# Four graph layers on one Trainium2 core: sums of layers 0 to 2 kept in PSUM, ScalarE's table row moved behind the next tile's hidden row, and layer 3's weighing done in the tile's own turn

## The chip, the cores and the metric

The kernel runs on one core of a Trainium2 chip. The metric is device time in microseconds, the median of the runs of one kernel. The profile is one execution; its times count from the first instruction.

## The reference

Four attention layers over 4096 nodes with 256 features share one sparse, symmetric adjacency matrix (about 9 neighbours a node, the node itself among them). Cut to what matters here:

```python
# each layer: h = relu(layernorm(x)); x = x + layer(h, adj, ...)
# layer 0 (4 heads): Wh = h @ W; e = leaky_relu(s_i[i] + s_j[j], 0.2), only where adj
out = elu(einsum('ijh,jhd->ihd', softmax(e, axis=1), Wh))
# layer 1 (1 head): h = node @ W; the same kind of scores, slope 0.01
out = h + softmax(e) @ node
# layer 2 (4 heads): as layer 0 with biases, no elu
out = einsum('hij,hjf->hif', softmax(S_masked), x_prime)
# layer 3 (4 heads): q, k, v = h @ Wq + bq, h @ Wk + bk, h @ Wv + bv
out = softmax(q @ k.T / 8 + mask) @ v
```

## The kernel before, in words

A first stage (266 us, not touched) turns the matrix into lists of neighbours and sorts the nodes by degree. From then on a tile is 128 nodes, one on each partition, and tile t takes `KS[t]` neighbours a node, from 23 for tile 0 down to 3 for tile 31: 276 in all. Layers 0 to 2 take the tiles in that order, layer 3 in the order `MIXED`, where long and short ones alternate (11, 11, 10, 10, 3, 5, 23, 9, 8, 5, 6, 9, 12, ... neighbours).

Every layer is a pipeline over 32 tiles:

- **POOL** gathers. One indirect DMA (line L749) fetches one neighbour's row for all 128 nodes, so that a layer has 276 of them. They land in a ring in SBUF (`s_ring`), where the tile's own row stands behind them: a tile with k neighbours has c = k + 1 rows. A tile's first gather waits until the tile whose room it takes is summed (semaphore `agg`). In layer 3 POOL also sends finished tiles home (L756), seven tiles behind its gathers, which waits for the tile's end (`x_new`).
- **VectorE (DVE)**, layers 0 to 2: scores (L1268 to L1272); in layer 0 then the places of the neighbours, in layer 1 a test of symmetry; the end of the tile before (`vec_finish`, L1427 to L1433: the sum is added to x) and its statistics (L1044 to L1049); the weights' normalising (L1300, L1307); and `vec_sum`, which multiplies the c rows by their weights (L1395), adds the upper half of the rows to the lower until two are left (L1399), and adds these into `s_half` (L1402). In layer 0 L1440 follows, which adds another product of the tile two before.
- **ScalarE (ACT)**, layers 0 to 2, for tile n: the exponentials (`act_exp`, L939), then `act_row(n-2)` (L916 to L930), which copies the next layer's projection of tile n-2 out of PSUM and stores it to the next layer's table in HBM, then `act_hidden(n-1)` (L877 to L895: layernorm and relu) and `act_turned(n-1)` (L904: copies the transposed row that TensorE made of it). In layer 0 `act_below` stands first.
- **TensorE (PE)**, layers 0 to 2: for each tile a transposition (L1555) and the projection (L1575 to L1586). In layer 2 this is layer 3's projection, k and v (L1575) and then q (L1580, L1581), whose PSUM bank must have been emptied by `act_row` of the tile before.
- **The next layer's first gathers** stand behind two waits: `EARLY` gathers of its first four tiles (24, before layer 3 20) go out when table rows up to tile 27 are stored, and take neighbours from these alone; the rest when all 32 tiles are.
- **Layer 3**: for tile n VectorE multiplies keys and query (`vec_dots`: L1284, L1286 and two small ones, the last L1290), then normalises and weighs tile n-1 (`vec_normal`, `vec_weigh`: L1300 to L1305, L1412 to L1417) and finishes tile n-2 (L1433). ScalarE runs the exponentials of tile n as soon as L1290 is done, then a copy of the query of tile n+2 (L957), and then weighs the first three rows of tile n-1 (`act_spare`, L967). TensorE adds the weighed rows of a tile in PSUM (L1600) and those three last (L1603), which raises `agg`.

All orders are written out by hand; no scheduler moves anything.

Of the kernel before, what the change touches and what calls it, by code (L numbers as in the profile page):

```python
# [9 lines left out]
ALU = mybir.AluOpType  # L10
# [453 lines left out]
class Sparse:  # L464
# [98 lines left out]
        return self.bank(4 if n % 2 == 0 else 6, 0, D)  # L563

    def total_y(self, L, n):
        return self.half[:, n % 2, :] if L.n < 3 else self.bank(2 + n % 2, 0, D)

    def landed(self, L, n):

# [400 lines left out]
    def act_layer(self, e, L):  # L970
        l = L.n + 1
        e.preload_act_table_set("natural_log_exp_and_others")
        if l == 1:
            e.wait_ge(self.ruled, 3 + len(set(KS)))
        if l == 4:
            self.act_asked(e, 0)
            self.act_asked(e, 1)
        for n in range(T):
            if n and l == 1:
                self.act_below(e, n - 1)  # L980
            self.act_exp(e, L, n)
            if l == 4:
                if n + 2 < T:
                    self.act_asked(e, n + 2)
                if n:
                    self.act_spare(e, n - 1)
                continue
            if n > 1:
                self.act_row(e, l, n - 2)
            if n:  # L990
                self.act_hidden(e, l, n - 1)
                self.act_turned(e, l, n - 1)
        if l == 1:
            self.act_below(e, T - 1)
        if l < 4:
            self.act_hidden(e, l, T - 1)
            self.act_row(e, l, T - 2)
            self.act_turned(e, l, T - 1)
            self.act_row(e, l, T - 1)
        else:  # L1000
            self.act_spare(e, T - 1)
# [417 lines left out]
    def vec_finish(self, e, L, n):  # L1419
# [22 lines left out]
    def vec_layer(self, e, L):  # L1442
# [301 lines left out]
```

## Time and profile before

| | |
|---|---|
| median of 3 runs | 1858.07 us (1850.53 to 1858.45) |
| the profiled execution: time, span | 1857.89 us, 1856.1 us |
| busy: POOL, DVE, PE, ACT | 1183.0, 1276.6, 724.0, 638.4 us |
| instructions on DVE, PE, ACT, POOL | 2730, 2660, 2069, 1201 |
| first stage | to 265.6 us |
| layer 0, layer 1, layer 2 (first to last gather) | 265.6 to 634.5, 637.8 to 1006.7, 1007.2 to 1374.9 us |
| layer 3 (first gather to the end) | 1403.9 to 1856.1 us |
| share of the chain that ended last: POOL, "issue" | 53%, 18% |

The busy time of an engine says how much it did, and the idle time before an instruction, with its releaser, what it waited for. "issue" is time between two instructions in which the profile shows no wait. A stage is bound by the engine that never waits in it, which need not be the busiest over the whole span.

### The profile page before, as it was taken

To read this page: it belongs to the slowest core of one execution; us is meant where nothing else is said; L and a number is where in the kernel's file an instruction comes from. 1 tells how busy PE (TensorE), PEld (TensorE's weight loads), DVE (VectorE), ACT (ScalarE), POOL (GpSimd) and SP (SyncE) were. 2 spreads that over 40 slices of the span, in tenths; PEclk is the share of its full clock that TensorE was granted. 3 is DMA by queue.
4 is the path that set the end of the run, shared out by engine and by line. 5 is a ranking of instruction groups with operands and counts; after the bars stand their busy time and mean duration, and the time that the engine had idled before them with its cause. 6 is when DMAs were issued, how large, how long until landed. Compare 5 with 4: busy or idle time off the path is not lost.

```text
span 1856.1 us, 12880 instructions
## 1 busy us (share of the span) xinstructions
PE 724.0 (39%) x2660; PEld 407.7 (22%) x2660; DVE 1276.6 (69%) x2730; ACT 638.4 (34%) x2069; POOL 1183.0 (64%) x1201
## 2 busy tenths in 40 slices
PE   3565500112223312233345134555666233455354
PEld 2443300001111101111122011222222222334243
DVE  2887743978888929666778196677653639668684
ACT  6778500223334511112223123233333222423343
POOL 0000267777777777777777787777744654777774
PEclk9996555555555555555555566666666566776777
DMA  9999789444454464444455644455545665777773
GB/s 354 384 384 364 183 278 169 107 117 119 125 133 129 129 135 110 123 128 124 131 142 135 135 119 141 138 151 152 161 137 158 193 167 160 232 239 223 240 233 101
DMA packets 171212, 328.63 MB, mean 177 GB/s; under 512 B 39918, under 2 KB 82935, under 8 KB 171128
## 3 DMA queue, kind: packets, MB, share of 16 engines
q0 software_dynamic: 65920, 197.88, 39.4%
q1 hardware_dynamic: 82600, 104.48, 17.6%
q10 hardware_dynamic: 22608, 25.40, 4.0%
q8 instruction: 23, 0.38, 0.1%
q14 instruction: 61, 0.50, 0.1%
HBM read 288.94 MB, written 38.72 MB: 177 GB/s over the span
## 4 chain that ended last, share of the span: by engine, by line
POOL 53%; issue 18%; PE 9%; DVE 8%; ACT 6%; DMA 4%; SPq 1%; ACTq 1%; POOLq 0%; DVEq 0%
POOL s_ring L749 50%; PE ps L1575 3%; ACT s_a L804 2%; DMA s_adj<-in_adj_dram 2%; DMA s_ring<-s_tab,s_idx 2%; PE ps L1544 2%; POOL s_pay L736 1%; DVE s_sc L1286 1%; DVE s_ring L1284 1%; POOL out_dram L756 1%; PE ps L1580 1%; SPq L599 1%; PE ps L1600 1%; DVE s_ring L1395 1%; DVE s_ring L1399 1%
## 5 line engine op out<-in xcount | busy, mean ns | idle before, releaser
L749 POOL DMA_INDIRECT s_ring<-s_tab,s_idx x1104 | 1115.6, 1010 | 419.3 <-issue 337.3
L939 ACT ACTIVATE ps<-s_sc,s_least 128x9 f32<-128x9 f32 (+12 forms) x416 | 110.3, 265 | 701.5 <-DVE s_least L1272 461.1
L1395 DVE TENSOR_TENSOR s_ring<-s_ring,ps 128x2304 f32<-128x2304 f32 (+10 forms) x96 | 261.2, 2720 | 3.3
L1399 DVE TENSOR_TENSOR s_ring<-s_ring 128x512 f32<-128x512 f32 (+7 forms) x249 | 234.8, 943 | 8.6
L1555 PE MATMUL ps<-s_ident,s_hb 128*128 128x128 f32 x128 | 43.8, 446 | 415.9 <-ACT s_hb L895 359.9
L1600 PE MATMUL ps<-s_ring,s_ident 128*128 128x256 f32 x366 | 125.2, 511 | 202.9 <-DVE s_ring L1417 202.9
L736 POOL DMA_INDIRECT s_pay<-s_pay_t,s_rank_i x32 | 31.2, 974 | 223.0 <-DVE s_rank_f L1144 213.5
L1284 DVE TENSOR_TENSOR s_ring<-s_ring,ps 128x2304 f32<-128x2304 f32 (+12 forms) x32 | 87.1, 2721 | 123.6 <-DMA s_ring<-s_tab,s_idx 123.2
L1268 DVE SCALAR_TENSOR_TENSOR s_sc<-s_ring 128x36 f32<-128x36 f32 (+20 forms) x96 | 18.4, 192 | 186.9 <-DMA s_ring<-s_tab,s_idx 186.6
L1584 PE MATMUL ps<-s_wx,s_hT 128*128 128x258 f32 (+1 forms) x256 | 134.8, 682 | 30.9 <-ACT s_hT L904 29.8
L1600 PEld LDWEIGHTS ps<-s_ring,s_ident 128*128 128x128 f32 x366 | 92.6, 261 | 232.5 <-issue 214.4
L1555 PE MATMUL ps<-s_ident,s_tb 128*128 128x128 f32 x64 | 22.1, 448 | 304.2 <-ACT s_tb L895 301.9
L1575 PE MATMUL ps<-s_wx,s_hT 128*128 128x512 f32 x128 | 118.9, 1084 | 16.7 <-ACT s_hT L904 16.2
L804 ACT ACTIVATE s_a<-s_adj 128x4096 fp8e4<-128x4096 int32 x32 | 115.4, 3610 | 14.9 <-DMA s_adj<-in_adj_dram 14.8
L1555 PEld LDWEIGHTS ps<-s_ident,s_hb 128*128 128x128 f32 x128 | 18.5, 203 | 445.6 <-ACT s_hb L895 388.7
L967 ACT ACTIVATE s_ring<-s_ring,s_few 128x64 f32<-128x64 f32 x384 | 94.5, 333 | 0.0
L1584 PEld LDWEIGHTS ps<-s_wx,s_hT 128*128 128x128 f32 x256 | 75.2, 324 | 69.0 <-ACT s_hT L904 54.6
L1286 DVE TENSOR_REDUCE s_sc<-s_ring 128x36 f32<-128x2304 f32 (+12 forms) x32 | 87.0, 2720 | 1.1
L1555 PEld LDWEIGHTS ps<-s_ident,s_tb 128*128 128x128 f32 x64 | 9.3, 204 | 326.8 <-ACT s_tb L895 326.8
L939 ACT ACTIVATION_READ_ACCUMULATOR ps<-s_sc,s_least 128x1 f32 x416 | 77.8, 187 | 0.0
L1544 PE MATMUL ps<-s_wx,s_hT 128*128 128x264 f32 x128 | 67.3, 681 | 18.2 <-ACT s_pay_t L865 16.8
L877 ACT ACTIVATE s_stat<-s_stat,s_eps 128x1 f32<-128x1 f32 x96 | 28.2, 294 | 106.0 <-DVE s_stat L1049 80.3
(190 smaller groups left out, 1409.3 us busy)
## 6 DMA issues: line engine op xcount, KB each, us to landing
s_adj<-in_adj_dram SPq DMA_DIRECT2D x32, 2048.0 KB, 16.1
s_ring<-s_tab,s_idx POOLq DMA_INDIRECT x1104, 3.2
s_tab<-s_tb ACTq DMA_DIRECT2D x32, 256.0 KB, 2.5
s_ring<-s_tab SPq DMA_DIRECT2D x32, 256.0 KB, 3.7
s_ring<-s_pay SPq DMA_DIRECT2D x32, 132.0 KB, 2.3
s_tab<-s_tb ACTq DMA_DIRECT2D x32, 132.0 KB, 2.5
s_ring<-s_tab SPq DMA_DIRECT2D x32, 132.0 KB, 2.3
s_tab<-s_tb ACTq DMA_DIRECT2D x32, 129.0 KB, 2.4
```

The costliest lines, as they stand in the source:

```text
L749: e.indirect_dma_start(g[:, k, 0:L.row], None, table, bass.IndirectOffsetOnAxis(ap=self.idx[:, t, k:k + 1], axis=0)).then_inc(self.gat[n % ...
L804: e.activation(self.a8[:, q % 2], self.adj[:, r], ACT.Copy, saturate=False).then_inc(self.conv)
L939: m = e.activation(p[:, :, h], s[:, :, h], ACT.Exp, bias=self.least[:, j, h:h + 1], scale=-1.0, accum_out=self.total[:, j, h:h + 1])
L967: m = e.activation(v, v, ACT.Copy, scale=p[:, k, h:h + 1])
L1284: e.tensor_tensor(keys, keys, wide(self.asked_for(n), 1, k + 1), ALU.mult).then_inc(self.v)
L1286: e.tensor_reduce(s, keys.rearrange("p k (h d) -> p k h d", h=4), AX, ALU.add).then_inc(self.v)
L1395: e.tensor_tensor(v, v, wide(p, 3, L.hd), ALU.mult).then_inc(self.v)
L1399: e.tensor_tensor(g[:, 0:h, :], g[:, 0:h, :], g[:, c - h:c, :], ALU.add).then_inc(self.v)
L1544: x = e.matmul(self.bank(7, 0, cols), self.hT[:, t % 2, k, :], self.wx[:, k, 0:cols], start=(k == 0), stop=(k == 1))
L1575: e.matmul(o, self.hT[:, j, k, :], self.wx[:, k, D:3 * D], start=(k == 0), stop=False)
L1584: x = e.matmul(o[:, 0:cols], self.hT[:, j, k, :], self.wx[:, k, 0:cols], start=(k == 0), stop=(k == 1 and l == 1))
L1600: e.matmul(y, self.ident[:], v, start=(k == SPARED), stop=False)
```

## The change

Three edits, the first on VectorE, the second on ScalarE, the third on VectorE:

1. In layers 0 to 2 the first two weighed rows are written to PSUM bank 2 (`two`, 512 columns), the others stay weighed in the ring. The ring's rows are then added to `two` one pair at a time. Layer 0 joins the two halves at the end; layers 1 and 2 leave them apart, and `vec_finish` adds them to x in two instructions.
2. `act_row(n-2)` stands behind `act_hidden(n-1)` and `act_turned(n-1)`.
3. In layer 3 a tile is `prompt` when the next one has eight gathers or more (19 of 32, the last among them): it is normalised and weighed right behind its own `vec_dots`, and finished behind the `vec_dots` of the next tile. The other 13 keep their order.

```diff
+HEAVY = 8
     def total_y(self, L, n):
-        return self.half[:, n % 2, :] if L.n < 3 else self.bank(2 + n % 2, 0, D)
+        return self.bank(2 if L.n < 3 else 2 + n % 2, 0, D)
+    def two(self):
+        return self.bank(2).rearrange("p (k d) -> p k d", k=2)
# act_layer
-            if n > 1:
-                self.act_row(e, l, n - 2)
             if n:
                 self.act_hidden(e, l, n - 1)
                 self.act_turned(e, l, n - 1)
+            if n > 1:
+                self.act_row(e, l, n - 2)
         if l < 4:
             self.act_hidden(e, l, T - 1)
+            self.act_turned(e, l, T - 1)
             self.act_row(e, l, T - 2)
-            self.act_turned(e, l, T - 1)
             self.act_row(e, l, T - 1)
# vec_sum
-        e.tensor_tensor(v, v, wide(p, 3, L.hd), ALU.mult).then_inc(self.v)
-        while c > 2:
-            e.wait_ge(self.v, vs.up())
-            h = c // 2
-            e.tensor_tensor(g[:, 0:h, :], g[:, 0:h, :], g[:, c - h:c, :], ALU.add).then_inc(self.v)
-            c -= h
-        e.wait_ge(self.v, vs.up())
-        e.tensor_tensor(self.half[:, n % 2, :], g[:, 0, :], g[:, 1, :], ALU.add).then_inc(self.agg)
+        e.tensor_tensor(parted(two), parted(g[:, 0:2, :]), wide(p[:, 0:2], 3, L.hd), ALU.mult).then_inc(self.v)
+        vs.up()
+        v = parted(g[:, 2:c, :])
+        e.tensor_tensor(v, v, wide(p[:, 2:c], 3, L.hd), ALU.mult).then_inc(self.v)
+        vs.up()
+        if c % 2:
+            e.wait_ge(self.v, vs.n)
+            e.tensor_tensor(two[:, 0, :], two[:, 0, :], g[:, c - 1, :], ALU.add).then_inc(self.v)
+            vs.up()
+            c -= 1
+        for a in range(2, c - 2, 2):
+            e.wait_ge(self.v, vs.n)
+            e.tensor_tensor(two, two, g[:, a:a + 2, :], ALU.add).then_inc(self.v)
+            vs.up()
+        e.wait_ge(self.v, vs.n)
+        if L.n:
+            e.tensor_tensor(two, two, g[:, c - 2:c, :], ALU.add).then_inc(self.agg)
+            return
+        e.tensor_tensor(g[:, c - 1, :], two[:, 1, :], g[:, c - 1, :], ALU.add).then_inc(self.v)
+        e.tensor_tensor(two[:, 0, :], two[:, 0, :], g[:, c - 2, :], ALU.add).then_inc(self.v)
+        vs.up()
+        e.wait_ge(self.v, vs.up())
+        e.tensor_tensor(two[:, 0, :], two[:, 0, :], g[:, c - 1, :], ALU.add).then_inc(self.agg)
# vec_finish, layer 1 (layer 2 alike, without total)
-            e.scalar_tensor_tensor(x, y, self.total[:, n % 2, 0:1], x, ALU.mult, ALU.add).then_inc(self.x_new)
+            e.scalar_tensor_tensor(x, y, total, x, ALU.mult, ALU.add).then_inc(self.v)
+            e.wait_ge(self.v, vs.up())
+            e.scalar_tensor_tensor(x, self.two()[:, 1, :], total, x, ALU.mult, ALU.add).then_inc(self.x_new)
+    def prompt(self, n):
+        return n == T - 1 or KS[MIXED[n + 1]] >= HEAVY
# vec_last
             self.vec_dots(e, n)
-            if n:
+            if n and not self.prompt(n - 1):
                 self.vec_normal(e, L, n - 1)
                 self.vec_weigh(e, n - 1)
-            if n > 1:
+            if n > 1 and not self.prompt(n - 2):
                 self.vec_finish(e, L, n - 2)
+            if n and self.prompt(n - 1):
+                self.vec_finish(e, L, n - 1)
+            if self.prompt(n):
+                self.vec_normal(e, L, n)
+                self.vec_weigh(e, n)
```

What this does to the instructions is seen at three places. Line numbers of the changed program are four or more higher.

VectorE before, layer 0, from the normalising of a tile with ten rows to the tile's end:

```order
L1307 TENSOR_TENSOR ps<-ps,s_total 128x40
L1395 TENSOR_TENSOR s_ring<-s_ring,ps 128x10x256
L1399 TENSOR_TENSOR s_ring<-s_ring 128x5x256
L1399 TENSOR_TENSOR s_ring<-s_ring 128x2x256
L1399 TENSOR_TENSOR s_ring<-s_ring 128x256
L1402 TENSOR_TENSOR s_half<-s_ring 128x256
L1440 TENSOR_TENSOR s_xs<-s_xs,ps 128x256
```

VectorE in the changed program, layer 0, the same place of such a tile (L1311 is the normalising, L1466 what was L1440):

```order
L1311 TENSOR_TENSOR ps<-ps,s_total 128x40
L1399 TENSOR_TENSOR ps<-s_ring,ps 128x512
L1402 TENSOR_TENSOR s_ring<-s_ring,ps 128x8x256
L1411 TENSOR_TENSOR ps<-ps,s_ring 128x512 x3
L1417 TENSOR_TENSOR s_ring<-ps,s_ring 128x256
L1418 TENSOR_TENSOR ps<-ps,s_ring 128x256
L1421 TENSOR_TENSOR ps<-ps,s_ring 128x256
L1466 TENSOR_TENSOR s_xs<-s_xs,ps 128x256
```

One multiplication and four additions have become two and six, and no addition reads two rows of SBUF any more.

ScalarE before, near the end of layer 2: the exponentials of tile 29 (six rows), and what stands behind them:

```order
L939 ACTIVATE ps,s_total<-s_sc,s_least 128x6 x4
L921 ACTIVATE s_tb<-ps 128x256
L922 ACTIVATE s_tb<-ps 128x512
L928 DMA s_tab<-s_tb 128x512
L930 DMA s_q<-s_tb 128x256
L877 ACTIVATE s_stat<-s_stat,s_eps 128x1
L879 ACTIVATE s_stat<-s_stat 128x1
L881 ACTIVATE s_stat<-s_stat 128x1
L895 ACTIVATE s_hb<-s_xs,s_stat 128x256
L904 ACTIVATE s_hT<-ps 128x256
```

ScalarE in the changed program, the same place:

```order
L943 ACTIVATE ps,s_total<-s_sc,s_least 128x6 x4
L881 ACTIVATE s_stat<-s_stat,s_eps 128x1
L883 ACTIVATE s_stat<-s_stat 128x1
L885 ACTIVATE s_stat<-s_stat 128x1
L899 ACTIVATE s_hb<-s_xs,s_stat 128x256
L908 ACTIVATE s_hT<-ps 128x256
L925 ACTIVATE s_tb<-ps 128x256
L926 ACTIVATE s_tb<-ps 128x512
L932 DMA s_tab<-s_tb 128x512
L934 DMA s_q<-s_tb 128x256
```

The copies and stores of tile 27 (two copies, two DMAs) have moved behind the hidden row of tile 28 and the copy of its transposition.

VectorE before, layer 3, the tile with 13 rows (place 12; place 11 in front of it has 10 rows, place 10 seven):

```order
L1284 TENSOR_TENSOR s_ring<-s_ring,ps 128x13x256
L1286 TENSOR_REDUCE s_sc<-s_ring 128x52
L1288 TENSOR_TENSOR s_sc<-s_sc,s_gap 128x48
L1290 TENSOR_REDUCE s_least<-s_sc 128x4
L1300 RECIPROCAL s_total<-s_total 128x4
L1304 TENSOR_TENSOR s_few<-ps,s_total 128x12
L1305 TENSOR_TENSOR ps<-ps,s_total 128x28
L1417 TENSOR_TENSOR s_ring<-s_ring,ps 128x4x256
L1417 TENSOR_TENSOR s_ring<-s_ring,ps 128x3x256
L1433 TENSOR_TENSOR s_xs<-s_xs,ps 128x256
```

VectorE in the changed program, the same tile (L1459 is the finish):

```order
L1288 TENSOR_TENSOR s_ring<-s_ring,ps 128x13x256
L1290 TENSOR_REDUCE s_sc<-s_ring 128x52
L1292 TENSOR_TENSOR s_sc<-s_sc,s_gap 128x48
L1294 TENSOR_REDUCE s_least<-s_sc 128x4
L1459 TENSOR_TENSOR s_xs<-s_xs,ps 128x256
L1304 RECIPROCAL s_total<-s_total 128x4
L1308 TENSOR_TENSOR s_few<-ps,s_total 128x12
L1309 TENSOR_TENSOR ps<-ps,s_total 128x40
L1436 TENSOR_TENSOR s_ring<-s_ring,ps 128x7x256
L1431 TENSOR_TENSOR s_ring<-s_ring,ps 128x3x256
L1433 TENSOR_REDUCE s_half<-s_ring 128x256
```

Before, the seven rows weighed here are those of place 11 (4 and 3), and the finish at the end is that of place 10. Now the finish comes first and is that of place 11, and the ten rows weighed behind it (7 and 3) are the tile's own.

## Rows read from the trace of the kernel before

**Rows 1.** Busy times by stage: stretch, us, PE, PEld, DVE, ACT, POOL (x instructions), clock, DMA.

```profile
265.60:634.50 368.90, 77.72 (x168) 41.01 (x168) 283.93 (x655) 113.66 (x466) 285.03 (x276) 0.50 0.55 137
1007.20:1374.90 367.70, 175.14 (x336) 70.36 (x336) 237.71 (x418) 109.87 (x428) 283.87 (x276) 0.63 0.53 144
```

**Rows 2.** Waits of POOL over the whole span: us in total, times, longest.

```profile
POOL s_ring L749 <- issue: 337.3, 1097, 3.4
POOL s_ring L749 <- DMA s_q<-s_tb: 42.3, 2, 29.0
```

**Rows 3.** The gathers' group on the page, and a stretch of the timeline (start, us).

```profile
L749 POOL DMA_INDIRECT s_ring<-s_tab,s_idx x1104 | 1115.6, 1010 | 419.3 <-issue 337.3
...
1209.00 2.82 DVE L1395 TENSOR_TENSOR s_ring<-s_ring,ps 128x2560 f32<-128x2560 f32 x1
...
1209.90 0.95 POOL L749 DMA_INDIRECT s_ring<-s_tab,s_idx  x1 [0.30 <-issue]
...
1211.86 2.68 DVE L1399 TENSOR_TENSOR s_ring<-s_ring 128x1280 f32<-128x1280 f32 x3
...
1212.40 1.76 POOL L749 DMA_INDIRECT s_ring<-s_tab,s_idx  x1 [0.30 <-issue]
```

**Rows 4.** VectorE's groups by form: times, busy us, mean ns of one, idle before.

```profile
L1402 DVE TENSOR_TENSOR s_half<-s_ring 128x256 f32<-128x256 f32 x96 | 40.8, 425 | 3.3
L1440 DVE TENSOR_TENSOR s_xs<-s_xs,ps 128x256 f32<-128x256 f32 x32 | 13.3, 415 | 4.7 <-ACT s_tb L916 4.7
L1417 DVE TENSOR_TENSOR s_ring<-s_ring,ps 128x512 f32<-128x512 f32 x15 | 9.9, 684 | 0.2
L1307 DVE TENSOR_TENSOR ps<-ps,s_total 128x40 f32<-128x40 f32 x8 | 1.7, 208 | 0.3
```

**Rows 5.** Waits of VectorE from 313.0 to 632.3 us (layer 0, tiles 0 to 28).

```profile
DVE s_sc L1268 <- DMA s_ring<-s_tab,s_idx: 26.4, 14, 4.0
```

**Rows 6.** Timeline at the change from layer 0 to layer 1.

```profile
634.31 0.33 ACTq L925 DMA_DIRECT2D s_tab<-s_tb  x1
...
637.82 0.38 ACT L904 ACTIVATE s_hT<-ps 128x256 f32<-128x256 f32 x1 [0.78 <-PE ps L1555]
637.84 1.59 POOL L749 DMA_INDIRECT s_ring<-s_tab,s_idx  x1 [3.37 <-issue]
```

**Rows 7.** Timeline of ScalarE near the end of layer 2.

```profile
1358.77 0.38 ACT L921 ACTIVATE s_tb<-ps 128x256 f32<-128x256 f32 x1 [4.69 <-PE ps L1581]
...
1362.80 0.38 ACT L904 ACTIVATE s_hT<-ps 128x256 f32<-128x256 f32 x1 [0.78 <-PE ps L1555]
...
1369.01 0.38 ACT L921 ACTIVATE s_tb<-ps 128x256 f32<-128x256 f32 x1 [4.68 <-PE ps L1581]
```

**Rows 8.** Timeline of POOL: layer 3's first gather, and its twenty-first.

```profile
1403.91 0.95 POOL L749 DMA_INDIRECT s_ring<-s_tab,s_idx  x1 [29.03 <-DMA s_q<-s_tb]
...
1442.07 0.94 POOL L749 DMA_INDIRECT s_ring<-s_tab,s_idx  x1 [13.29 <-DMA s_q<-s_tb]
```

**Rows 9.** Timeline in layer 3 around the end of one tile's `vec_dots`.

```profile
1700.50 0.28 ACT L939 ACTIVATE ps<-s_sc,s_least 128x9 f32<-128x9 f32 x1 [7.74 <-DVE s_least L1290]
...
1701.99 2.96 ACT L967 ACTIVATE s_ring<-s_ring,s_few 128x64 f32<-128x64 f32 x12
...
1709.52 1.46 PE L1603 MATMUL ps<-s_ring,s_ident 128*128 128x256 f32 x6
```

**Rows 10.** VectorE in layer 3: waits from 1452.3 us, the first, the longest of the rest, the last.

```profile
DVE s_ring L1284 <- DMA s_ring<-s_tab,s_idx: 123.2, 19, 32.6
DVE s_xs L1433 <- PE ps L1603: 9.1, 3, 3.6
...
1452.28 3.35 DVE L1284 TENSOR_TENSOR s_ring<-s_ring,ps 128x3072 f32<-128x3072 f32 x1 [32.58 <-DMA s_ring<-s_tab,s_idx]
...
1533.89 6.55 DVE L1284 TENSOR_TENSOR s_ring<-s_ring,ps 128x6144 f32<-128x6144 f32 x1 [28.44 <-DMA s_ring<-s_tab,s_idx]
...
1843.48 0.42 DVE L1433 TENSOR_TENSOR s_xs<-s_xs,ps 128x256 f32<-128x256 f32 x1 [2.67 <-PE ps L1603]
```

More of the change, by code:

```diff
@@ L1388, in vec_sum @@
         vs, g, p = self.vs, self.rows(L, n)[:, :, 0:D], self.scores(L, n)[1]
-        c = KS[L.order[n]] + 1
+        c, two = KS[L.order[n]] + 1, self.two()
+        parted = lambda a: a.rearrange("p k (h d) -> p k h d", h=L.heads)
         if L.n == 1:
@@ L1393, in vec_sum @@
             e.wait_ge(self.normal, self.normals(L, n))
-        v = g.rearrange("p k (h d) -> p k h d", h=L.heads)
-        e.tensor_tensor(v, v, wide(p, 3, L.hd), ALU.mult).then_inc(self.v)
-        while c > 2:
-            e.wait_ge(self.v, vs.up())
-            h = c // 2
-            e.tensor_tensor(g[:, 0:h, :], g[:, 0:h, :], g[:, c - h:c, :], ALU.add).then_inc(self.v)
-            c -= h
+        e.tensor_tensor(parted(two), parted(g[:, 0:2, :]), wide(p[:, 0:2], 3, L.hd), ALU.mult).then_inc(self.v)
[19 more added lines that the diff above has]
+        vs.up()
         e.wait_ge(self.v, vs.up())
-        e.tensor_tensor(self.half[:, n % 2, :], g[:, 0, :], g[:, 1, :], ALU.add).then_inc(self.agg)
+        e.tensor_tensor(two[:, 0, :], two[:, 0, :], g[:, c - 1, :], ALU.add).then_inc(self.agg)
     def vec_weigh(self, e, n):
@@ L1430, in vec_finish @@
         elif L.n == 1:
-            e.scalar_tensor_tensor(x, y, self.total[:, n % 2, 0:1], x, ALU.mult, ALU.add).then_inc(self.x_new)
+            total = self.total[:, n % 2, 0:1]
+            e.scalar_tensor_tensor(x, y, total, x, ALU.mult, ALU.add).then_inc(self.v)
+            e.wait_ge(self.v, vs.up())
+            e.scalar_tensor_tensor(x, self.two()[:, 1, :], total, x, ALU.mult, ALU.add).then_inc(self.x_new)
+        elif L.n == 2:
+            e.tensor_tensor(x, x, y, ALU.add).then_inc(self.v)
+            e.wait_ge(self.v, vs.up())
+            e.tensor_tensor(x, x, self.two()[:, 1, :], ALU.add).then_inc(self.x_new)
         else:
@@ L1475, in vec_last @@
             self.vec_dots(e, n)
-            if n:
+            if n and not self.prompt(n - 1):
                 self.vec_normal(e, L, n - 1)
                 self.vec_weigh(e, n - 1)
-            if n > 1:
+            if n > 1 and not self.prompt(n - 2):
                 self.vec_finish(e, L, n - 2)
-        self.vec_normal(e, L, T - 1)
-        self.vec_weigh(e, T - 1)
-        self.vec_finish(e, L, T - 2)
+            if n and self.prompt(n - 1):
[3 more added lines that the diff above has]
+                self.vec_weigh(e, n)
+        if not self.prompt(T - 2):
+            self.vec_finish(e, L, T - 2)
         self.vec_finish(e, L, T - 1)
```

## The prediction

> **What bounds the kernel now.** I read the busy times by stage first. In layer 0 and in layer 2 POOL runs 276 gathers in 368.9 and 367.7 us with 285.0 and 283.9 us of busy time [rows 1]; layer 1 reads like layer 0. Then POOL's waits: nearly all of its idle time is "issue", 337.3 us in 1,097 pieces of 0.3, which is the price of the next gather, not a wait [rows 2]. So layers 0 to 2 run at POOL's pace. A free gather takes 0.95 us and 0.30 of issue, 1.25 together [rows 3]; 276 of them are 344.6 us. What is above that is in long gathers: 1,104 took 1115.6 us [rows 3], which is 72 more than 1,104 x 0.945. The timeline shows when. A gather that starts while L1395 multiplies (one operand in SBUF, one in PSUM) takes 0.95; the one that started at 1212.40, half a microsecond into the three L1399 additions (both operands in SBUF), took 1.76 [rows 3]. The first of the three (1280 columns, 1.49 us at 960 columns a us and 0.15 fixed) ends at 1213.35, the gather 0.81 later. I laid all gathers over the instruction that VectorE runs 0.13 us after their start: under L1399 112 of 132 are long, and each ends 0.82 us after that addition; under L1395 none of 206. Some 68 of the 72 us lie under L1399 and L1402, 24 us of it in each of layers 0 and 1 and 23 in layer 2.
>
> One other place costs POOL time before layer 3. Between layers 2 and 3 it waits 29.03 and 13.29 us for stored table rows [rows 8], 42.3 in all [rows 2].
>
> **Edit 1, the sums.** On POOL it takes away what holds the gathers: the additions read one operand from PSUM. The form "PSUM from PSUM and SBUF" exists before, as L1307 [rows 4], and none of the 9 gathers over it was long. I take 70 of 72 us as gone; layer 0's L1429 (two SBUF operands) keeps about 1.
>
> On VectorE it costs. An operand in PSUM is no dearer: 256 columns take 415 ns with it and 425 without [rows 4], 512 take 684 [rows 4]. L1307, which writes PSUM, takes 208 ns for 40 columns [rows 4]: 166 fixed, where the 684 hold 151. The Trainium skill, "VectorE: DVE Perf Modes", its section on the TRN2 errata, gives an operation from PSUM 62 cycles more of fixed cost than one from SBUF; at its 0.96 GHz that would be 65 ns each and, over some 200 additions up to tile 28, 13 us more in layer 0. The rows show no such difference. The sum goes by the rows. Ten rows before: 2.82 for the multiplication, 2.68 for three additions [rows 3], 0.42 for L1402, some 6.0 with gaps. After, in layer 0: 0.68 and 2.28 (8 rows, 0.15 + 8 x 0.267), three times 0.68, three times 0.42, with gaps 6.6; two pairs do not wait for each other and overlap by 0.12, so +0.3. Twenty-four rows give +1.4, thirteen +0.7, six +0.1. Over tiles 0 to 28 that is +12.8 us in layer 0 and +10.8 in layers 1 and 2 (second addition in the finish included).
>
> Layer 2 has room for it (VectorE busy 238 of 368 us [rows 1]), and layer 1 nearly as much. Layer 0 has not (284 of 369 [rows 1], much of the rest at its start). VectorE starts its first tile at 313.0, 18 us behind the gathers, and up to tile 29's scores (632.3) it waited for gathers 26.4 us [rows 5] of 319.3. With 12.8 more work and no waits that stretch is 305.2 us: tile 29 starts at 618.2, and POOL, done at 610, waits. **Layer 0 becomes VectorE's.**
>
> **Edit 2, ScalarE's order.** It moves two things in opposite ways. The row of tile 27, for which the next layer's first gather waits, now stands behind hidden and turned row of tile 28. In layer 0 its DMA was issued at 634.31, 3.5 us before POOL's first gather of layer 1 (637.84), and the copy L904 that will precede it ended at 638.20 [rows 6]: 4.1 us later. So layer 1 starts at 618.2 + (638.4 - 632.3) + 3.5 = 627.8, where it was 637.8: 10 us gained of the 24. POOL then has 24 early gathers (30 us) before it needs the last rows, which are there. Layer 1: 344.6 us, then a wait of about 3 for tile 27's row (2.7 later by the same count, where POOL arrived just in time): layer 2 starts at 975.5, before 1007.2.
>
> Near the end of layer 2 the old order is a ring: copy of tile n-2's projection, hidden row n-1, its transposition, 5.8 us of projection on PE (1363.18 to 1369.01), and again the copy, which waits 4.69 for it; 10.24 us a tile [rows 7], where the gathers need 8.7 to 3.8. This ring is why POOL waits 42.3 us. In the new order the copy comes when the projection is already done, and PE goes on at once: 5.7 + 0.78 + 0.38 = 6.9 us a tile [rows 7]. From tile 27 on this is a little slower than the gathers. Its row arrives about 5 us after POOL's last gather of layer 2, the last row 1.5 us after the 20 early ones. So 42.3 becomes about 6.5. Layer 3's twenty-first gather then goes out at 975.5 + 344.6 + 5 + 25 + 1.5 = 1351.6, before 1442.1: **90 us ahead**.
>
> **Edit 3, layer 3.** What is queued behind what decides it. `vec_finish(n-1)` now stands before `vec_normal(n)` and waits until tile n-1 is summed. That needs `act_spare(n-1)`, which ScalarE still runs behind the exponentials of tile n, and these wait for `vec_dots(n)`. So the finish cannot start until dots(n) is over and then exponentials, query copy and spare are: 1700.50 to 1704.95, 4.45 us (4.4 to 4.6 in 25 of the 31 tiles that have such a pair), then three matmuls of 1.46 together [rows 9]: 6.1 us in which VectorE stands still. Before, normalising and weighing the last tile covered it; now nothing does. This happens for 18 tiles (all prompt ones but the last): 110 us. Behind it stand the tile's own weighing and all later dots.
>
> VectorE's layer 3 from its first dots (1452.28) to its last finish (1843.48) was 391.2 us, of which it waited 123.2 - 32.6 = 90.6 for gathers and 9.1 for sums [rows 10], so 291.5 of work. New: 291.5 + 110 + 1.5 (first exponentials) + 25 for tile 6 (its ring space comes free when tile 2 is summed, so the 28.4 [rows 10] stay nearly whole) + 5 at the end = 433. A tile with nine rows then takes VectorE some 14 us (twice 2.55 for the dots and 0.4 for the small ones, 6.1, 0.4 for the finish, twice 0.95 and 0.4 for the weighing) against 10.0 for its 8 gathers and one DMA home, so no further wait for gathers hides in it. **Layer 3 becomes VectorE's, 42 us longer.** Ring space freed earlier brings nothing, since POOL no longer leads.
>
> **Sum.** 1351.6 + 10.2 (first landing) + 433 + 12.6 (last finish to the end) = 1807.4 us span, 49 less than 1856.1. The profiled execution took 1.8 more than its span and lies 0.2 below the median of the runs, so I forecast 1809 us.
>
> **Rivals.**
> - *The finish does not stand in layer 3* (ScalarE's part done earlier than I read it). Layer 3 stays POOL's at best: 42 less, 1767. Against it: the order of the three engines. 8%.
> - *The gathers stay held* (an addition with one SBUF operand still takes what a gather reads): the 70 us stay, VectorE's additions are more, only the end of layer 2 gains some 36, layer 3 loses 42, and the stretch before loses a few: about 1870, slower than before. It decides as soon as more than two thirds of the 72 us stay. Against it: 9 short gathers over L1307, 206 over L1395. 6%.
> - *PSUM operands are dearer than the rows say*, as by the rule above. Every 0.05 us on an addition is 10 us in layer 0, while layers 1 and 2 hide it; layer 3 is untouched. No row before shows 512 columns written to PSUM; the bounds from the nearest ones are 0 (L1440 against L1402) and 0.015 (L1307's fixed part), and only a price outside them makes this case: at 0.1 us, 1829. 9%. By the 62 cycles of the Trainium skill ("VectorE: DVE Perf Modes", the TRN2 errata) it would be 1822.
> - *The reorder on ScalarE pays little* because PE's projection slows or tile 27's row comes later than I count: 42 stays half or whole, 1825 to 1845. 8%.
>
> **How the numbers follow.** My forecast as a whole has 69%, with its own range 1792 to 1826: layer 0 +-6, end of layer 2 +-5, layer 3 +-12 (each finish +-0.6). The range 1782 to 1840 leaves out the first two rivals and the worst of the last. A change within 0.5% (1849 to 1867) can hardly be told from none. Faster by over 0.5%: 0.90; within: 0.04; slower: 0.06.
>
> **What would show it.** Long gathers gone in layers 0 to 2 (276 in 285 us of busy time becomes 261). In layer 0 no wait of VectorE for gathers and one of some 18 us of POOL before layer 1. Table row waits before layer 3 of about 5 and 1.5. In layer 3 L1459 with about 18 waits of 6 us for PE's last matmuls, VectorE's dots no longer waiting. It is wrong if those waits are missing, or if gathers over L1411 are long.

## The result, and the profile after

The changed kernel takes 1834.43 us (median of 4 runs, 1831.8 to 1836.44) where the kernel before takes 1857.61 beside it: a ratio of 0.9883, 95% interval 0.9855 to 0.991. That is 23 us less. I had forecast 1809, 49 less. The sign and the stated range (1782 to 1840) held. The gain is a little under half of what I forecast, and the time lies outside the range of the forecast itself (1792 to 1826).

Each time below stands beside that of the kernel before, taken with it; where that is 2135 to 2155 us in place of 1856 to 1858, instructions come late (the last section), so that such a time is compared with its neighbour alone and only waits and durations are read from its trace.

In the page's groups of the changed kernel (busy us, mean ns of one, idle before) the first two rows answer to [rows 3, 4], the third to [rows 10]:

```profile
L753 POOL DMA_INDIRECT s_ring<-s_tab,s_idx x1104 | 1046.3, 948 | 446.4 <-issue 346.8
...
L1411 DVE TENSOR_TENSOR ps<-ps,s_ring 128x512 f32<-128x512 f32 x246 | 171.9, 699 | 8.5
...
L1459 DVE TENSOR_TENSOR s_xs<-s_xs,ps 128x256 f32<-128x256 f32 x32 | 13.4, 418 | 143.7 <-PE ps L1637 143.6
```

The 1,104 gathers have a mean of 948 ns, the free gather's length: of the 72 us of holding 3 are left. The busy times of layers 0 and 2, in the columns of [rows 1]:

```profile
266.20:611.50 345.30, 74.86 (x162) 39.43 (x162) 286.81 (x735) 107.67 (x441) 261.47 (x276) 0.50 0.58 145
975.20:1321.30 346.10, 173.70 (x367) 70.10 (x368) 256.85 (x518) 119.44 (x463) 262.32 (x276) 0.67 0.57 156
```

POOL's 276 gathers take 345 and 346 us where they took 369 and 368 [rows 1], with 261 and 262 us of busy time. The starts of layers 1, 2 and 3 and layer 3's twenty-first gather, in POOL's timeline:

```profile
626.82 0.94 POOL L753 DMA_INDIRECT s_ring<-s_tab,s_idx  x1 [15.35 <-issue]
...
975.21 0.94 POOL L753 DMA_INDIRECT s_ring<-s_tab,s_idx  x1 [3.42 <-DMA s_tab<-s_tb]
...
1324.85 0.94 POOL L753 DMA_INDIRECT s_ring<-s_tab,s_idx  x1 [3.52 <-DMA s_q<-s_tb]
...
1349.84 0.94 POOL L753 DMA_INDIRECT s_ring<-s_tab,s_idx  x1 [0.31 <-issue]
```

I had 627.8, 975.5 and, for the last, 1351.6. POOL stands 15.35 us at the end of layer 0, because that layer is VectorE's now (from 313 to 618 us VectorE waits for no gather, where it waited 26.4 us [rows 5]), and the waits of 29.03 and 13.29 us [rows 8] are 3.52 and 0.31. Up to here the forecast is within 2 us, and the kernel is 92.2 us ahead. The rest is lost in layer 3. Its waits of VectorE (us in total, times, longest), and a stretch of the timeline that answers to [rows 9]:

```profile
DVE s_xs L1459 <- PE ps L1637: 143.6, 22, 9.3
DVE s_ring L1288 <- DMA s_ring<-s_tab,s_idx: 48.8, 2, 26.6
```

```profile
1665.40 0.22 DVE L1294 TENSOR_REDUCE s_least<-s_sc 128x4 f32<-128x36 f32 x1
1665.65 0.28 ACT L943 ACTIVATE ps<-s_sc,s_least 128x9 f32<-128x9 f32 x1 [13.52 <-DVE s_least L1294]
...
1666.83 0.36 ACT L961 ACTIVATE ps<-s_ring 128x256 f32<-128x256 f32 x1
1667.14 2.96 ACT L971 ACTIVATE s_ring<-s_ring,s_few 128x64 f32<-128x64 f32 x12
1670.15 2.93 PE L1637 MATMUL ps<-s_ring,s_ident 128*128 128x256 f32 x6 [6.67 <-ACT s_ring L971]
1673.11 0.42 DVE L1459 TENSOR_TENSOR s_xs<-s_xs,ps 128x256 f32<-128x256 f32 x1 [7.50 <-PE ps L1637]
```

The chain is the one that I described: dots of the next tile, its exponentials, a query copy, ScalarE's three rows (4.45 us from 1665.65 to 1670.10), the three matmuls, the finish. But the matmuls take 2.93 us, not 1.46, and the finish waits 7.50, not 6.1. All 18 prompt tiles show 2.93; 17 of their waits are 7.24 to 7.54 us, one is 9.28, 135.5 together. VectorE's layer 3, from its first dots (1359.91) to its last finish (1820.15), is 460.2 us where I had 433 and where it was 391.2.

### The profile page after: what moved, and what is told of

Its sections match the earlier page's. It is cut to its first block, busy times and chain, and to the rows that moved or that the text cites. A ratio compares the mean times of both kernels' runs of the same rounds, so it can differ in the third digit from the quotient of the medians.

```text
span 1833.3 us, 13149 instructions
## 1 busy us (share of the span) xinstructions
PE 720.6 (39%) x2660; PEld 412.1 (22%) x2660; DVE 1307.3 (71%) x2999; ACT 636.9 (35%) x2069; POOL 1113.8 (61%) x1201
## 4 chain that ended last, share of the span: by engine, by line
DVE 31%; POOL 29%; issue 15%; ACT 9%; PE 8%; DMA 5%; SPq 2%; ACTq 0%; POOLq 0%; DVEq 0%
POOL s_ring L753 27%; DVE s_sc L1290 4%; DVE s_ring L1288 4%; DVE s_ring L1402 4%; DVE ps L1411 3%; PE ps L1637 3%; ACT s_ring L971 3%; ACT s_a L808 3%; SPq L603 2%; DMA s_adj<-in_adj_dram 2%; PE ps L1578 2%; DVE s_ring L1436 2%; DMA s_ring<-s_tab,s_idx 2%; POOL s_pay L740 2%; DVE ps L1399 1%
## 5 line engine op out<-in xcount | busy, mean ns | idle before, releaser
L753 POOL DMA_INDIRECT s_ring<-s_tab,s_idx x1104 | 1046.3, 948 | 446.4 <-issue 346.8
L1402 DVE TENSOR_TENSOR s_ring<-s_ring,ps 128x1792 f32<-128x1792 f32 (+10 forms) x96 | 209.2, 2179 | 0.0
L1411 DVE TENSOR_TENSOR ps<-ps,s_ring 128x512 f32<-128x512 f32 x246 | 171.9, 699 | 8.5
L1634 PE MATMUL ps<-s_ring,s_ident 128*128 128x256 f32 x366 | 125.5, 512 | 114.2 <-DVE s_ring L1436 114.2
L1637 PE MATMUL ps<-s_ring,s_ident 128*128 128x256 f32 x192 | 75.2, 550 | 160.4 <-ACT s_ring L971 160.4
L1634 PEld LDWEIGHTS ps<-s_ring,s_ident 128*128 128x128 f32 x366 | 95.9, 268 | 147.3 <-issue 127.5
L1288 DVE TENSOR_TENSOR s_ring<-s_ring,ps 128x2304 f32<-128x2304 f32 (+12 forms) x32 | 86.9, 2716 | 49.1 <-DMA s_ring<-s_tab,s_idx 48.8
L1459 DVE TENSOR_TENSOR s_xs<-s_xs,ps 128x256 f32<-128x256 f32 x32 | 13.4, 418 | 143.7 <-PE ps L1637 143.6
L1609 PE MATMUL ps<-s_wx,s_hT 128*128 128x512 f32 x128 | 104.7, 965 | 15.2 <-ACT s_hT L908 14.7
L1637 PEld LDWEIGHTS ps<-s_ring,s_ident 128*128 128x128 f32 x192 | 50.1, 274 | 178.5 <-ACT s_ring L971 169.6
```

What stands on the lines that cost most here:

```text
L753: e.indirect_dma_start(g[:, k, 0:L.row], None, table, bass.IndirectOffsetOnAxis(ap=self.idx[:, t, k:k + 1], axis=0)).then_inc(self.gat[n % ...
L1288: e.tensor_tensor(keys, keys, wide(self.asked_for(n), 1, k + 1), ALU.mult).then_inc(self.v)
L1402: e.tensor_tensor(v, v, wide(p[:, 2:c], 3, L.hd), ALU.mult).then_inc(self.v)
L1411: e.tensor_tensor(two, two, g[:, a:a + 2, :], ALU.add).then_inc(self.v)
L1609: e.matmul(o, self.hT[:, j, k, :], self.wx[:, k, D:3 * D], start=(k == 0), stop=False)
L1634: e.matmul(y, self.ident[:], v, start=(k == SPARED), stop=False)
```

## The experiments

**Edits 1 and 2 without 3** (layer 3 in the order of before):

```diff
     def vec_last(self, e, L):
         for n in range(T):
             self.vec_dots(e, n)
-            if n and not self.prompt(n - 1):
+            if n:
                 self.vec_normal(e, L, n - 1)
                 self.vec_weigh(e, n - 1)
...
```

> The changed kernel with layer 3's order of before (edits 1 and 2 alone). If edit 3 costs what the trace after shows (layer 3 from its first dots to its last finish 460 us where it was 391), this kernel is faster than both: 21st gather of layer 3 at about 1350, then 10.2 + 391 + 12.6, span 1764, time 1766. If instead layer 3 became longer because it starts with POOL earlier or because POOL's gathers there meet something new, the order of before would not help and the time stays near 1834.

For the second run:

> The same kernel as the first (edits 1 and 2 alone), once more, since on that chip the kernel before took 2138 us where it had 1858, with stretches in which VectorE got an instruction only every 0.7 us. If the kernel before runs at 1858 here, layer 3's order of before gives 1766 with edits 1 and 2. If the kernel before is at 2138 again, it is again near 2120.

Measured: 1765.79 us beside 1856.48, ratio 0.9509 (0.9489 to 0.953); the first run was 2119.89 beside 2137.86. VectorE's waits in layer 3:

```profile
DVE s_ring L1288 <- DMA s_ring<-s_tab,s_idx: 116.4, 19, 27.8
DVE s_xs L1459 <- PE ps L1633: 8.5, 3, 3.0
```

They are those of [rows 10]: gathers lead again, and the sums are waited for three times. The twenty-first gather went out at 1351.88, and the last finish ended 399.8 us later (401.8 before, 470.7 in the changed kernel). So edit 3 turns a gain of 91 us into one of 23, and the step that sized edits 1 and 2 (90 us) was right.

**Edit 3 without 1 and 2** (the kernel before with `prompt` and the new `vec_last`):

> The kernel before with edit 3 alone. If layer 3's new order makes VectorE stand 7.5 us at 18 finishes whatever comes ahead, layer 3 is 460 us here too: 1442 + 10 + 460 + 13 = 1925 span, time 1927. By the prediction's own sum (6.1 us a finish, 433) it would be 1900. If edit 3 only hurts together with edits 1 and 2, it is near 1858.

Measured: 2223.9 us beside 2137.86, ratio 1.0418 (1.037 to 1.0465), so the time where the kernel before takes 1857 us stays open. The waits can be read; two of VectorE's finishes in layer 3:

```profile
1721.86 0.42 DVE L1434 TENSOR_TENSOR s_xs<-s_xs,ps 128x256 f32<-128x256 f32 x1 [7.51 <-PE ps L1612]
...
1739.32 0.42 DVE L1434 TENSOR_TENSOR s_xs<-s_xs,ps 128x256 f32<-128x256 f32 x1 [7.51 <-PE ps L1612]
```

The 7.5 us are there without edits 1 and 2 (14 of the waits are 7.24 to 7.54). They are a price of the order alone. Ten other waits are shorter or longer than that, up to 24 us.

**Edit 1 without 2 and 3:**

> The kernel before with edit 1 alone. Theory: gathers of layers 0 to 2 free (0.95 us), layer 1 starts near 624, layer 2 near 969; then the ring of 10.24 us a tile at the end of layer 2 stays and takes some 12 of the 23 us back there; 21st gather of layer 3 near 1393, time 1809 (49 less than before). POOL's wait for table rows grows from 42 to over 50. Rival: the ring takes all of it back, since it began before the gathers were held: 1820 to 1830.

For the two runs after it, the last the one that counts:

> The kernel before with edit 1 alone. Where the kernel before takes 1858: gathers of layers 0 to 2 free, layer 1 starts near 624, layer 2 near 969, the ring of 10.24 us a tile at the end of layer 2 stays and takes some 12 of the 23 us back there, 21st gather of layer 3 near 1393, 1809. Rival, the ring takes all of layer 2's gain back: 1820 to 1830. Where the kernel before takes 2138, it is near 2156.

> The kernel before with edit 1 alone. Where the kernel before takes 1858: gathers of layers 0 to 2 free, layer 1 starts near 624, layer 2 near 969, the ring of 10.24 us a tile at the end of layer 2 stays and takes some 12 of the 23 us back there, 21st gather of layer 3 near 1393, 1809. Rival, the ring takes all of layer 2's gain back: 1820 to 1830. Where the kernel before takes 2138, it is near 2156.

Measured: 1798.06 us beside 1856.44, ratio 0.9688 (0.9671 to 0.9706); twice before 2155.83 and 2154.67 beside 2138 and 2137. POOL's waits for table rows before layer 3:

```profile
1341.83 0.95 POOL L752 DMA_INDIRECT s_ring<-s_tab,s_idx  x1 [28.22 <-DMA s_q<-s_tb]
...
1379.98 0.94 POOL L752 DMA_INDIRECT s_ring<-s_tab,s_idx  x1 [13.42 <-DMA s_q<-s_tb]
```

Layers 1 and 2 start at 620.51 and 966.57, as expected within 4 us, but the twenty-first gather goes out 13 us earlier than I expected: the waits are those of [rows 8] to within 1 us, so the faster gathers did not run further into ScalarE's and TensorE's ring at the end of layer 2. My count of a loss of 12 us there was wrong. Edit 1 is worth 58 us and edit 2 on top of it 32 (1798 to 1766, both beside 1856).

**Edit 2 without 1 and 3:**

> The kernel before with edit 2 alone. Theory: layers 1 and 2 start 4 and some 7 us later, the wait for table rows before layer 3 falls from 42 to about 6, 21st gather near 1415, time 1831. Rival: PE's projection or the hidden row stays the ring and the wait stays above 20: 1845 or more.

Measured: 2100.49 us beside 2137.86, ratio 0.9814 (0.9765 to 0.9863): faster, but its size where the kernel before takes 1857 us is open. POOL's waits for table rows before layer 3 are 45.2 us in this run, so it does not show the fall to 6 us that I expected. The runs beside 1856 us show it: 41.6 us with edit 1 alone, 3.9 with edits 1 and 2.

**The running sums in SBUF.** The changed kernel, the same instructions, the sums in `s_half`:

```diff
     def total_y(self, L, n):
-        return self.bank(2 if L.n < 3 else 2 + n % 2, 0, D)
+        return self.half[:, 0, :] if L.n < 3 else self.bank(2 + n % 2, 0, D)
     def two(self):
-        return self.bank(2).rearrange("p (k d) -> p k d", k=2)
+        return self.half[:]
```

> The changed kernel with the two running sums in SBUF (s_half) in place of PSUM bank 2; the same instructions, both operands of each addition in SBUF again. If two SBUF operands are what holds a gather, gathers over L1411 are long again, less than before since each addition is only 0.7 us long: 30 to 60 us of busy time above the free gathers in layers 0 to 2, of which layer 0 hides its part; time 1850 to 1865. If only the length and shape of the old additions held them, gathers stay at 0.95 and the time at 1834.

Measured: 2192.62 us beside 2134.95, ratio 1.0255 (1.0206 to 1.0303); whether it takes 1850 to 1865 us where the kernel before takes 1857 stays open. The gathers can be read. POOL's and VectorE's groups, and the timeline of additions and gathers in layer 0:

```profile
L753 POOL DMA_INDIRECT s_ring<-s_tab,s_idx x1104 | 1073.5, 972 | 764.2 <-issue 387.7 <-PE ps L1637 134.3 <-DVE s_half L1415 89.4
L1411 DVE TENSOR_TENSOR s_half<-s_half,s_ring 128x512 f32<-128x512 f32 x246 | 170.6, 693 | 33.6 <-DVE s_half L1411 18.9 <-issue 3.7 <-DVE s_half L1406 3.2
```

```profile
426.50 1.42 DVE L1411 TENSOR_TENSOR s_half<-s_half,s_ring 128x512 f32<-128x512 f32 x2
426.76 1.25 POOL L753 DMA_INDIRECT s_ring<-s_tab,s_idx  x1 [0.30 <-issue]
428.11 0.69 DVE L1411 TENSOR_TENSOR s_half<-s_half,s_ring 128x512 f32<-128x512 f32 x1 [0.20 <-issue]
428.31 1.31 POOL L753 DMA_INDIRECT s_ring<-s_tab,s_idx  x1 [0.30 <-issue]
```

Gathers over L1411 are long again, 69 of 99, and each ends 0.82 us after the addition that it started under. In the changed kernel a like stretch of layer 0 has four additions in a row and every gather at 0.95:

```profile
394.00 2.90 DVE L1411 TENSOR_TENSOR ps<-ps,s_ring 128x512 f32<-128x512 f32 x4
395.11 0.94 POOL L753 DMA_INDIRECT s_ring<-s_tab,s_idx  x1 [0.30 <-issue]
396.36 0.95 POOL L753 DMA_INDIRECT s_ring<-s_tab,s_idx  x1 [0.30 <-issue]
```

None of the 136 gathers over L1411 is long in the changed kernel, and none of 103 in the first run of edits 1 and 2 alone (2119.89), so late instructions are not the reason. The second operand's place is what frees the gathers, not the shape of the additions. The excess over 0.95 us in layers 0 to 2 is 25 us, under the 30 to 60 that I expected, against 70 before: an addition of 0.69 us holds a gather less long than one of 1.49. By the Trainium skill, "SBUF — State Buffer", the section on who interferes with whom, an instruction of VectorE with two SBUF inputs contends with an instruction of GpSimd that reads SBUF; the trace agrees, as far as the gather is one, since its indices (`s_idx`) lie in SBUF. The rows also price the sum's place itself: 699 ns in PSUM against 693 here, and 433 against 426 for L1421, with nothing else changed. That is 6 to 7 ns. The Trainium skill, "VectorE: DVE Perf Modes", its section on the TRN2 errata, which the prediction weighed, has 62 cycles more for an operation from PSUM, an estimate of 65 ns; the trace does not agree.

**ScalarE's three rows at once.** The changed kernel, with ScalarE weighing them behind a prompt tile's own exponentials:

```diff
                 if n + 2 < T:
                     self.act_asked(e, n + 2)
-                if n:
+                if n and not self.prompt(n - 1):
                     self.act_spare(e, n - 1)
+                if self.prompt(n):
+                    self.act_spare(e, n)
                 continue
...
-        else:
-            self.act_spare(e, T - 1)
```

> The changed kernel with ScalarE weighing the first three rows of a prompt tile behind its own exponentials, ahead of those of the next tile. Theory: a finish then finds its sum ready (no waits at L1459), what stays is 19 waits of 1.5 us for the exponentials ahead of the normalising (28 us); VectorE needs some 350 and POOL leads; ring room comes free earlier by one tile's dots, so 1735 to 1766, about 1750. If the prediction's reading of the order were wrong and the waits had another cause, L1459 waits stay.

For the three runs after it, the last the one that counts:

> The changed kernel with ScalarE weighing the first three rows of a prompt tile behind its own exponentials, ahead of those of the next tile; once more, on a chip where the kernel before should take 1858. Theory: a finish then finds its sum ready (no waits at L1459), what stays is 19 waits of 1.5 us for the exponentials ahead of the normalising (28 us); VectorE needs some 350 and POOL leads; ring room comes free earlier by one tile's dots, so 1735 to 1766, about 1750. If the prediction's reading of the order were wrong and the waits had another cause, L1459 waits stay and the time is near 1834.

> The changed kernel with ScalarE weighing the first three rows of a prompt tile behind its own exponentials, ahead of those of the next tile. Where the kernel before takes 1858: no waits at L1459, 19 waits of 1.4 us for the exponentials at L1304 instead (28 us), POOL leads layer 3 again, 1735 to 1766, about 1750. Rival, the waits at L1459 have another cause: near 1834. Where the kernel before takes 2138, it is at 2120 to 2128 as twice before and tells nothing of the size.

> The changed kernel with ScalarE weighing the first three rows of a prompt tile behind its own exponentials, ahead of those of the next tile. Where the kernel before takes 1858: no waits at L1459, 19 waits of 1.4 us for the exponentials at L1304 instead (28 us), POOL leads layer 3 again, 1735 to 1766, about 1750. Rival, the waits at L1459 have another cause: near 1834. Where the kernel before takes 2138 it tells nothing of the size.

Measured: 1753.94 us beside 1856.79, ratio 0.9449 (0.9433 to 0.9465); three times before 2120.29, 2128.65 and 2124.86 beside 2135 to 2139. The end of one tile's dots in layer 3:

```profile
1566.79 0.26 DVE L1294 TENSOR_REDUCE s_least<-s_sc 128x4 f32<-128x60 f32 x1
1566.96 0.41 DVE L1459 TENSOR_TENSOR s_xs<-s_xs,ps 128x256 f32<-128x256 f32 x1
...
1568.50 0.18 DVE L1304 RECIPROCAL s_total<-s_total 128x4 f32<-128x4 f32 x1 [1.13 <-ACT ps L943]
...
1568.92 2.97 ACT L971 ACTIVATE s_ring<-s_ring,s_few 128x64 f32<-128x64 f32 x12 [0.25 <-DVE s_few L1308]
...
1576.67 1.46 PE L1637 MATMUL ps<-s_ring,s_ident 128*128 128x256 f32 x6
```

The finish (L1459) finds its sum ready and starts at once; what stays is the wait of 1.13 us for the exponentials. Over layer 3 the waits at L1459 fall from 143.6 to 10.9 us, and those for the exponentials at L1304 are ten of 0.3 to 1.4 us, 9.2 together, where I expected 19 and 28 us. The three matmuls come right behind TensorE's other rows and take 1.46. VectorE waits for gathers again (91.8 us at L1288), and the ring's waits of POOL fall from 85.1 to 19.6 us. One edit on ScalarE is worth 80 us, and the prompt order, which cost 69, now gains 12 against the order of before (1765.79).

**TensorE kept busy.** The changed kernel, with 12 more matmuls into an unused bank for each prompt tile from the third on:

```diff
+        if n > 1 and n < T - 1 and self.prompt(n):
+            for k in range(12):
+                if k == 6:
+                    e.wait_ge(self.scored, 3 * T + n + 2)
+                e.matmul(self.bank(5, 0, D), self.ident[:], g[:, SPARED, D:2 * D], start=True, stop=True)
         e.wait_ge(self.spared, n + 1)
```

> The changed kernel with 12 matmuls more for each prompt tile, into an unused PSUM bank: six behind the weighed rows, six when the next tile's dots are done, ahead of the last three. They only keep TensorE busy. If the prediction's finish wait was too small because TensorE, idle for 6 to 10 us, runs the last three matmuls at its lower clock (2.93 us where the row had 1.46), L1637 falls back to 1.46 and each of 18 waits from 7.5 to 6.0: 27 us less, 1807. If the clock isn't the cause, L1637 stays at 2.93 and the time at 1834 or above.

For the two runs after it:

> The changed kernel with 12 matmuls more for each prompt tile into an unused PSUM bank, six behind the weighed rows, six when the next tile's dots are done. Where the kernel before takes 1858: the last three matmuls (L1642) 1.56 us in place of 2.93, the finish waits 6.1 in place of 7.5 for most of 18 tiles, 1834 less 18 x 1.4 = 1809, the forecast. If the wait's size has nothing to do with TensorE's clock, 1834 or more. Where the kernel before takes 2138, only the durations can be read.

> The changed kernel with 12 matmuls more for each prompt tile into an unused PSUM bank. Where the kernel before takes 1858: the last three matmuls (L1642) 1.56 us in place of 2.93, the finish waits 6.1 in place of 7.5 for most of 18 tiles, 1834 less 18 x 1.4 = 1809, the forecast. If the wait's size has nothing to do with TensorE's clock, 1834 or more. Where the kernel before takes 2138, only the durations can be read.

Measured: 2214.08 us beside 2143.7, ratio 1.0334 (1.027 to 1.0397); twice before 2211.68 and 2210.31 beside 2135. Whether it takes the time to 1809 is open. The durations are plain. Tile 1 has no added matmuls, tile 2 has them (L1639); the last three matmuls are L1642:

```profile
1710.26 2.93 PE L1642 MATMUL ps<-s_ring,s_ident 128*128 128x256 f32 x6 [6.34 <-ACT s_ring L971]
1713.22 0.42 DVE L1459 TENSOR_TENSOR s_xs<-s_xs,ps 128x256 f32<-128x256 f32 x1 [7.51 <-PE ps L1642]
...
1721.08 5.34 PE L1639 MATMUL ps<-s_ring,s_ident 128*128 128x256 f32 x24
...
1727.73 1.56 PE L1642 MATMUL ps<-s_ring,s_ident 128*128 128x256 f32 x6 [1.31 <-ACT s_ring L971]
1729.33 0.42 DVE L1459 TENSOR_TENSOR s_xs<-s_xs,ps 128x256 f32<-128x256 f32 x1 [6.14 <-PE ps L1642]
```

The same two stretches by window (the clock is the third number from the end):

```profile
1710.30:1713.20 2.90, 2.89 (x6) 1.80 (x6) 0.00 (x0) 0.00 (x0) 0.00 (x0) 0.50 0.00 0
1727.75:1729.25 1.50, 1.50 (x6) 1.03 (x6) 0.00 (x0) 0.00 (x0) 0.00 (x0) 1.00 0.00 0
```

At a granted clock of 0.50 (1.2 GHz) the three matmuls take 2.93 us and the finish waits 7.51; at 1.00 (2.4 GHz) they take 1.56 and it waits 6.14, which is the 6.1 that the prediction had. This holds for most prompt tiles with added matmuls: ten of 16 have 1.56, the other six more, two of them 2.93.

**The finish behind the weighing.** The changed kernel, where `vec_finish(n-1)` follows the weighing of a prompt tile n and no longer stands ahead of it:

> The changed kernel with the finish of tile n-1 behind the weighing of a prompt tile n, not ahead of it. If the loss is that nothing covers ScalarE's and TensorE's part, the finish then waits about 3 us (7.5 less 1.5 of wait for the exponentials moved ahead, 0.8 of normalising and 2 of weighing) for 18 tiles, VectorE's layer 3 falls from 460 to 380 to 395, and POOL leads again: 1765 to 1775. If the weighing at once is itself what costs, it stays above 1810.

For the second run:

> The changed kernel with the finish of tile n-1 behind the weighing of a prompt tile n. Where the kernel before takes 1858: the wait for the exponentials (1.4 us) comes out at the normalising, and the finish then waits 3 us in place of 7.5; VectorE's layer 3 falls from 460 to 380 to 395 us and POOL leads again, 1765 to 1775. If the weighing at once is itself what costs, above 1810. Where the kernel before takes 2138, only the waits can be read.

Measured: 2168.41 us beside 2134.95 and 2184.49 beside 2154.9, ratios 1.0168 (1.0105 to 1.0231) and 1.0136 (1.01 to 1.0172). The wait for the exponentials comes out at the normalising, 1.34 to 1.45 us in 11 tiles, as expected. Of 28 waits at the finish in each run 20 are 0.3 to 4.3 us (I expected 3), but eight are 4.9 to 29 us, and that these hold the late instructions of such runs is not shown. Inconclusive: what covering the wait on VectorE alone is worth stays open.

**ScalarE's new order in layer 2 alone**, with the three rows at once:

```diff
+            if n > 1 and l < 3:
+                self.act_row(e, l, n - 2)
             if n:
                 self.act_hidden(e, l, n - 1)
                 self.act_turned(e, l, n - 1)
-            if n > 1:
+            if n > 1 and l == 3:
                 self.act_row(e, l, n - 2)
```

> The kernel with ScalarE's three rows at once (1754), and ScalarE's new order in layer 2 alone, the old one in layers 0 and 1. The row of tile 27 is stored 4 us earlier at the end of layer 0, and 3 us earlier at the end of layer 1, where POOL waits for it: layer 3 starts 7 us earlier, 1747. Rival: POOL's arrival, not the row, sets the start of layer 2, and only the 4 us of layer 0 show: 1750. Where the kernel before takes 2138, only the starts of the layers can be read.

Measured: 1747.82 us beside 1856.17, ratio 0.9416 (0.9388 to 0.9443), the fastest of all. POOL's first gathers of layers 1 and 2:

```profile
622.08 0.94 POOL L753 DMA_INDIRECT s_ring<-s_tab,s_idx  x1 [10.96 <-issue]
...
969.01 0.94 POOL L753 DMA_INDIRECT s_ring<-s_tab,s_idx  x1 [2.13 <-DMA s_tab<-s_tb]
```

The end of each layer, behind the last tile, keeps the new order. The gathers were at 625.72 and 974.71 with the order new everywhere: 3.6 us at the end of layer 0 (I had 4.1) and 2.1 more at the end of layer 1 (I had 2.7).

## Why the prediction missed, point by point

- **What bounds the kernel, and edit 1 on POOL: right.** Of the 72 us of holding 69 are gone (I had 70), and the reason is shown, not only argued: the same instructions with two SBUF operands hold the gathers again.
- **Edit 1 on VectorE: right.** Tile 29's scores start at 618.33 (I had 618.2; the terms of that sum, 319.3 less 26.4 plus 12.8, add up to 0.5 more), an addition of 512 columns takes 699 ns (I had 684), POOL waits at the end of layer 0 (15.35 us, I had some 18). The rival of dearer PSUM operands falls with 6 to 7 ns.
- **Edit 2: right.** Waits of 3.5 and 0.3 us before layer 3 (I had 5 and 1.5), and its small costs in layers 0 and 1 are there.
- **Edit 3: the mechanism right, the size wrong.** The term is "then three matmuls of 1.46 together [rows 9]: 6.1 us in which VectorE stands still". They take 2.93, the wait is 7.5. Over 18 tiles that is 135.5 us where I had 110: 25.5 of the 25.9 us by which the span (1833.3) is above my 1807.4. The other differences nearly cancel: the twenty-first gather 1.8 earlier, tile 6's wait for gathers 22.2 in place of 25, four waits at other finishes 8.0 in place of the 5 at the end, and under 2 us more work of VectorE.
- **Why the term was off.** I took the duration from a row in which TensorE had just been adding that tile's other rows, so its clock was up. In the new order it has stood idle for 5.0 to 10 us by then (30 in one tile) and runs the three at 0.50. Here are the three matmuls of the tile above by window, in the columns of [rows 1]:

```profile
1670.15:1673.05 2.90, 2.90 (x6) 1.85 (x6) 0.00 (x0) 0.00 (x0) 2.29 (x3) 0.50 0.52 164
```

  The matmuls added ahead of them bring back 1.56 and 6.14. My bound on this term, "each finish +-0.6", was no bound. The trace of before held the other end of it, in a tile where TensorE had been idle for 15.68 us, ran four passes (2.04 us, a granted clock of 0.50) and was still at 0.50 for the last three matmuls; the next tile's have 1.46 again (TensorE's timeline):

```profile
1760.40 2.04 PE L1600 MATMUL ps<-s_ring,s_ident 128*128 128x256 f32 x4 [15.68 <-DVE s_ring L1417]
1764.00 2.93 PE L1603 MATMUL ps<-s_ring,s_ident 128*128 128x256 f32 x6 [1.55 <-ACT s_ring L967]
...
1772.18 1.46 PE L1603 MATMUL ps<-s_ring,s_ident 128*128 128x256 f32 x6
```

  With the 2.93 us in the sum the wait is 7.6 us and the forecast span 1834.
- **The rivals.** "The finish does not stand in layer 3", 1767, did not happen, but the two versions that remove the wait land on its side: 1766 without edit 3, 1754 with ScalarE's rows at once. The other three did not happen: gathers over L1411 are not long, an operand in PSUM costs 6 to 7 ns, and the waits for table rows are gone. The measured 1834 lies within the 1825 to 1845 of the last of them, but by chance: the mechanism is another.

## What to carry to other kernels

A wait moved to a new place takes the durations of its new place with it: a matmul read where TensorE is busy cost double here behind 5 us or more of idle time, so price each term of a new wait at both clocks. When an instruction is to run earlier on one engine, follow all engines that feed it: weighing a tile at once gained nothing, and cost 69 us, as long as ScalarE still did its three rows behind the next tile's exponentials; moved along, it gained 12. And where VectorE adds two rows of SBUF while POOL issues indirect DMAs, try one operand in PSUM: here edit 1 was worth 58 us.

## What the runs showed of the hardware that I had not expected

- An addition of VectorE to a sum in PSUM costs 6 to 7 ns more than the same to a sum in SBUF (699 against 693 ns for 512 columns, 433 against 426 for 256; the other operand is in SBUF in both).
- In some runs VectorE's instructions come late. Six chips showed it and two of them showed the usual case too. The kernel before takes 15% longer then, and the three kernels with edit 1 that were timed in both cases 20 to 21%, so a ratio from there is not that of the usual case. This is VectorE in one of them, layer 0 (ScalarE's rows at once):

```profile
404.11 0.17 DVE L1327 TENSOR_SCALAR s_met_at<-s_place 128x13 f32<-128x13 f32 x1 [1.22 <-DVE s_place L1325]
406.21 0.17 DVE L1331 TENSOR_TENSOR s_met_at<-s_met_at,s_place 128x13 f32<-128x13 f32 x1 [1.92 <-remote]
407.61 0.27 DVE L1333 TENSOR_SCALAR s_over<-s_met_at 128x6 f32<-128x6 f32 x1 [1.23 <-DVE s_met_at L1331]
409.01 0.17 DVE L1335 TENSOR_SCALAR s_met_at<-s_met_at 128x6 f32<-128x6 f32 x1 [1.13 <-DVE s_over L1333]
409.71 0.17 DVE L1337 CAST s_idx<-s_met_at 128x13 int32<-128x13 f32 x1 [0.53 <-DVE s_met_at L1335]
```

  They start 0.70, 1.40 or 2.10 us apart, where the same lines elsewhere follow each other in 0.2. Single instructions last the same: a free gather 0.95 us, an addition at L1411 699 ns. Edit 1, which adds 269 instructions on VectorE and gains 3.1% elsewhere, measures 0.8 and 0.9% slower in such runs (1.0084 and 1.0091). Neither the cause of the lateness was tried nor whether the number of instructions is why edit 1 loses by it.
